# One mixer kernel, one change: half of the clamped differences through PSUM, one transpose bank instead of two, and another written order of the work

## The chip, the core and the metric

The kernel runs on one core of one Trainium2 chip. The metric is the device time of one execution in microseconds (us), lower is better. The engines of the core work side by side, each through its own list of instructions: PE (TensorE, matmuls; PEld is its weight load), DVE (VectorE), ACT (ScalarE), POOL (GpSimd) and SP (SyncE, which issues the DMAs). They meet only through semaphores.

## The reference

An input of 8 sequences of 256 tokens with 256 features is normalised to `xn`, and then `out = x + mamba_mixer(xn) + mlp(xn)`. The mixer, cut to what matters here (64 heads of 64 channels, state size 128):

```python
z, xbc, dt = split(xn @ W_in)              # 4096 + 4352 + 64 columns
xbc = silu(causal_conv1d(xbc, 4 taps))     # x: 4096 channels, B and C: 128 each
dt = softplus(dt + dt_bias); dA_cs = cumsum(dt * A)
L[i, j, h] = exp(dA_cs[i, h] - dA_cs[j, h])  for j <= i, else 0
Y[i, h] = sum_j (C_i . B_j) * L[i, j, h] * dt[j, h] * x[j, h]
y = (Y + D * x) * silu(z)
out_mixer = rmsnorm(y) * norm_w @ W_out
```

The MLP behind it is 6 blocks of two matmuls with a Gelu and a layernorm. It is the same before and after.

## The kernel before

Three stages follow each other. `prepare` (0 to about 72 us) normalises the input, computes B, C, the decay sums and `gmat`, the masked products C.B per sequence. `mix` (72 to 1040 us) is the stage that the change touches. `mlp` (from 1042 us) is the rest.

`mix` works through 32 channel tiles of 128 channels (2 heads each). A tile `c` has all 2048 tokens, in 4 blocks `b` of 512 tokens; a block is 2 sequences, and such a sequence is a *unit* `s` (0 or 1). For a tile the work is:

- PE `project_x`, `project_z` (8 products of 6 matmuls, L501) into the banks `pa0`, `pa1`.
- ACT `conv0` (L817) takes the x product out of PSUM, DVE `tap` (L517) adds three more taps per block from PSUM; then the bank is free and ACT `silu_x` (L826) finishes the block. ACT `silu_z` (L835) takes the z product out and frees its bank.
- PE `tokens` (L721) transposes a block of x into a bank `pt`, ACT `copy_tokens` (L862) copies it to `xtok`.
- DVE `exponents` (L943), per unit: 2 heads by 2 pieces of 256 and 128 columns, so 4 instructions, each `max(srow - stok, -CAP)`, SBUF to SBUF. ACT `decays` (L844) takes the exponential of the unit, POOL `times_g` (L657) multiplies it by `gmat`.
- PE `outputs` (L740), per unit: `xtok` times the unit's weights into `py`. DVE `add_dx` (L957) and `gate` (L971) finish the block; ACT `square` (L853) and POOL `add_square` (L666) gather the sum of squares.
- PE `output_rows` (L758), 4 calls per tile, multiplies the gated channels of a finished pair of tiles by `W_out` into `po`; DVE `add_rows` (L984) adds them to `acc`.

The order on each engine is written out by hand: a function `step(c)` per engine, called for c = -2 to 34. In a step an engine does parts of tile c, c-1 and c+1 in the order in which the calls stand; waits on semaphores inside the calls do the rest. An engine never passes an instruction that waits. Exp and Silu need different function tables on ACT; going from one to the other costs an ACT_TABLE_LOAD. `stok` (L923) is a small copy of the tile's columns of `tokpar`, made once per tile on DVE.

Two places of the code matter for the argument: `decays` and `silu_x`/`silu_z` in ACT's `step`, whose sequence sets how many table loads there are, and `outputs` in PE's `step`.

Of the kernel before, what the change touches and what calls it, by code (L numbers as in the profile page):

```python
# [28 lines left out]
P = 128  # L29
# [502 lines left out]
def mix(nc, w_xz, conv_par, d_par, w_out, w1, cs_dram, ident, xhi, xlo, acc, gmat, tokpar,  # L532
# [13 lines left out]
    with ExitStack() as ctx:  # L546
# [4 lines left out]
        stok = sb("stok", [P, 2, TILES, HPT])  # L551

        oraw = sb("oraw", [P, 2, DM + 1])
        osc = sb("osc", [P, 2, DM])
# [7 lines left out]
        pt = [ps(f"pt{i}") for i in range(2)]  # L562
        py = [ps(f"py{i}") for i in range(2)]
        po = [ps(f"po{i}") for i in range(2)]

# [67 lines left out]
        @block.gpsimd  # L633
        def _(pool):
            pool.memset(sqacc[:], 0.0).then_inc(pool_set, 1)
            pool.memset(onesq[:], 1.0).then_inc(pool_set, 1)
            pool.wait_ge(pool_set, 2)

            def w_lo(c):
                if not 2 <= c < NCT:  # L640
                    return
                t = tile_of(c)

# [24 lines left out]
            def step(c):  # L669
                add_square(c - 1, 1)  # L670
                times_g(c, 1, 0)
                times_g(c, 1, 1)
                times_g(c, 2, 0)
                add_square(c - 1, 2)
                times_g(c, 2, 1)
                add_square(c - 1, 3)
                times_g(c, 3, 0)
                w_lo(c + 2)
                times_g(c, 3, 1)
                times_g(c + 1, 0, 0)  # L680
                times_g(c + 1, 0, 1)
                add_square(c, 0)

            steps(step)

        @block.tensor
        def _(pe):
# [24 lines left out]
            def tokens(c, b):  # L712
# [47 lines left out]
                last.then_inc(o_done, 1)  # L760

            def step(c):
                project_x(c, 1)
                output_rows(c - 1, 0)
                outputs(c - 1, 0, 1)
                output_rows(c - 1, 1)
                project_x(c, 2)
                tokens(c - 1, 2)
                outputs(c - 1, 1, 0)
                outputs(c - 1, 1, 1)  # L770
                tokens(c - 1, 3)
                output_rows(c - 1, 2)
                project_x(c, 3)
                outputs(c - 1, 2, 0)
                output_rows(c - 1, 3)
                project_z(c, 0)
                outputs(c - 1, 2, 1)
                project_z(c, 1)
                project_z(c, 2)
                project_z(c, 3)  # L780
                outputs(c - 1, 3, 0)
                outputs(c - 1, 3, 1)
                tokens(c, 0)
                project_x(c + 1, 0)
                tokens(c, 1)
                outputs(c, 0, 0)

            steps(step)

            pe.wait_ge(sq_added, NB * NCT)  # L790
            for t in range(TILES):
                last = pe.matmul(pt[0][:, t:t + 1], sqacc[:, t * P:(t + 1) * P], onesq[:, 0:1],
                                 start=True, stop=True)
            last.then_inc(ms_done, 1)

# [1 line left out]
        def _(act):  # L797
# [57 lines left out]
            def copy_tokens(c, b):  # L855
                if not 0 <= c < NCT:
# [5 lines left out]
                act.copy(xtok[:, b % 2].rearrange("p t c -> p (t c)"), pt[b % 2][:]  # L862
                         ).then_inc(xtok_copied, 1)

            def scale_o(c):
# [7 lines left out]
                                   scale=oraw[:, e, DM:DM + 1]).then_inc(o_scaled, 1)  # L873

            def step(c):
                silu_z(c, 0)
                silu_x(c, 1)
                silu_x(c, 2)
                scale_o(c - 1)
                silu_z(c, 1)  # L880
                silu_z(c, 2)
                silu_x(c, 3)
                square(c - 1, 0)
                silu_z(c, 3)
                decays(c, 0, 0)
                decays(c, 0, 1)
                w_hi(c + 2)
                copy_tokens(c, 0)
                decays(c, 1, 0)
                decays(c, 1, 1)  # L890
                square(c - 1, 1)
                conv0(c + 1, 0)
                conv0(c + 1, 1)
                decays(c, 2, 0)
                copy_tokens(c, 1)
                conv0(c + 1, 2)
                copy_tokens(c, 2)
                decays(c, 2, 1)
                decays(c, 3, 0)
                square(c - 1, 2)  # L900
                copy_tokens(c, 3)
                square(c - 1, 3)
                conv0(c + 1, 3)
                decays(c, 3, 1)
                silu_x(c + 1, 0)

            steps(step)

# [1 line left out]
        def _(dve):  # L910
# [7 lines left out]
                conv_tap(dve, xt[:, t.par, cols(b)], pa[b % 2][:],  # L918
                         conv[:, t.par, TAPS - 1 - k:TAPS - k], k).then_inc(done, 1)

            def s_by_tokens(t):
                wait_past(dve, arg_done, SPB * NB * (t.c - 1))
                dve.tensor_copy(stok[:, t.par], tokpar[:, :, bass.ds(HPT * t.c, HPT)]  # L923
                                ).then_inc(stok_done, 1)

            def exponents(c, b, s):
                if not 0 <= c < NCT:
# [2 lines left out]

                m = SPB * (NB * t.c + b) + s
                half, i0 = b // 2, b % 2 * BLK + s * SEQ
                if b == 0 and s == 0:
                    s_by_tokens(t)
                    dve.wait_ge(stok_done, t.c + 1)
# [12 lines left out]
            def add_dx(c, b):  # L948
# [35 lines left out]
                dve.tensor_tensor(rows, po[i][:], rows, ALU.add).then_inc(o_added, 1)  # L984

            def step(c):
                add_rows(c - 1, 2)
                tap(c, 2, 2)
                tap(c, 3, 1)
                tap(c, 2, 3)  # L990
                tap(c, 3, 2)
                add_dx(c - 1, 1)
                tap(c, 3, 3)
                gate(c - 1, 1)
                add_rows(c - 1, 3)
                add_dx(c - 1, 2)
                gate(c - 1, 2)
# [5 lines left out]
                add_dx(c - 1, 3)  # L1003
                tap(c + 1, 0, 2)
                tap(c + 1, 1, 1)
                tap(c + 1, 1, 2)
                add_rows(c, 0)
                tap(c + 1, 0, 3)
                gate(c - 1, 3)
                exponents(c, 2, 0)  # L1010
                exponents(c, 2, 1)
                add_dx(c, 0)
                tap(c + 1, 1, 3)
                exponents(c, 3, 0)
                exponents(c, 3, 1)
                gate(c, 0)
                tap(c + 1, 2, 1)
                add_rows(c, 1)

            steps(step)  # L1020

            dve.wait_ge(ms_done, 1)
            dve.tensor_scalar(meansq[:], pt[0][:, 0:TILES], 1.0 / DI, EPS, ALU.mult,
                              ALU.add).then_inc(ms_copied, 1)

# [487 lines left out]
```

## Time and profile before

| | |
|---|---|
| median of 3 runs | 1621.53 us (1615.85 to 1621.72) |
| the profiled execution | 1617.42 us, its span 1615.4 us, mean granted TensorE clock 0.984 |
| busy share of the span | PE 93%, PEld 74%, DVE 74%, ACT 63%, POOL 58% |
| `mix` | about 72 to 1040 us, 32 tiles |
| one tile (step) in `mix` | 29.58 us, the mean of 31 |

In a timeline row "x8" means that eight neighbouring instructions of one kind are merged; the distance from its start to the start of the next row is the time which the engine gave to all eight.

### The profile page before, as it was taken

To read this page: it belongs to the slowest core of one execution; us is meant where nothing else is said; L and a number is where in the kernel's file an instruction comes from. 1 tells how busy PE (TensorE), PEld (TensorE's weight loads), DVE (VectorE), ACT (ScalarE), POOL (GpSimd) and SP (SyncE) were. 2 spreads that over 40 slices of the span, in tenths; PEclk is the share of its full clock that TensorE was granted. 3 is DMA by queue.
4 is the path that set the end of the run, shared out by engine and by line. 5 is a ranking of instruction groups with operands and counts; after the bars stand their busy time and mean duration, and the time that the engine had idled before them with its cause. 6 is when DMAs were issued, how large, how long until landed. Compare 5 with 4: busy or idle time off the path is not lost. (4 is left out here: it accounts for less than half of the span.)

```text
span 1615.4 us, 25959 instructions
## 1 busy us (share of the span) xinstructions
PE 1496.2 (93%) x8920; PEld 1200.1 (74%) x8920; DVE 1199.4 (74%) x2565; ACT 1019.4 (63%) x1620; POOL 938.8 (58%) x619
## 2 busy tenths in 40 slices
PE   6678999999999999999999998999999999999998
PEld 4556667666667666676666666789998998999988
DVE  7878788788788787887887887356676677677752
ACT  6557767767767677677676775366555555555542
POOL 4256677667766776776677667563535263343560
PEclk9889999999999999999999999899999999999999
DMA  4322223223232222222332311220100101020011
GB/s 134 105 85 99 66 86 99 66 85 99 70 103 76 92 86 72 92 86 73 97 93 70 108 65 53 71 74 1 63 1 27 36 0 62 0 75 0 0 53 40
DMA packets 50152, 107.52 MB, mean 67 GB/s; under 512 B 13249, under 2 KB 25793, under 8 KB 48449
## 3 DMA queue, kind: packets, MB, share of 16 engines
q1 hardware_dynamic: 50048, 106.21, 20.6%
q8 instruction: 57, 0.93, 0.2%
q14 instruction: 47, 0.38, 0.1%
HBM read 101.47 MB, written 4.72 MB: 66 GB/s over the span
## 5 line engine op out<-in xcount | busy, mean ns | idle before, releaser
L657 POOL TENSOR_TENSOR mix_dec<-mix_dec,gmat 128x768 f32<-128x768 f32 x256 | 466.6, 1836 | 222.4 <-ACT mix_dec L844 222.4
L517 DVE SCALAR_TENSOR_TENSOR xt<-mix_pa,conv,xt 128x510 f32<-128x510 f32 x372 | 263.9, 735 | 140.5 <-ACT xt L817 139.3
L1365 DVE TENSOR_TENSOR mlp_hlo<-mlp_h,mlp_hhi 128x512 fp32r<-128x512 f32 x192 | 208.2, 1086 | 184.8 <-ACT mlp_hhi L1297 184.6
L844 ACT ACTIVATE mix_dec<-mix_dec 128x768 f32<-128x768 f32 x256 | 209.6, 842 | 188.8 <-DVE mix_dec L943 188.3
L943 DVE TENSOR_SCALAR mix_dec<-srow,mix_stok 128x256 f32<-128x256 f32 (+1 forms) x1024 | 260.8, 327 | 27.0 <-PE mix_py L740 23.1
L740 PE MATMUL mix_py<-mix_dec,mix_xtok 128*64 128x256 f32 (+1 forms) x2048 | 213.3, 340 | 68.6 <-POOL mix_dec L657 36.9
L1292 ACT ACTIVATE mlp_h<-mlp_p,mlp_b1c 128x512 f32<-128x512 f32 x192 | 132.0, 687 | 203.7 <-PE mlp_p L501 197.8
L740 PEld LDWEIGHTS mix_py<-mix_dec,mix_xtok 128*64 128x64 f32 x2048 | 130.4, 138 | 166.8 <-ACT mix_xtok L862 81.9
L758 PE MATMUL mix_po<-mix_osc,mix_yg 128*128 128x256 f32 x1024 | 250.0, 389 | 0.0
L501 PE MATMUL mix_pa<-xhi,whi 128*128 128x512 f32 x496 | 220.7, 445 | 16.2 <-DVE xt L517 16.2
L1258 PE MATMUL mlp_p<-mlp_w2hi,mlp_hhi 128*128 128x256 f32 x768 | 218.7, 285 | 3.2 <-DVE acc L1424 3.2
L1260 PE MATMUL mlp_p<-mlp_w2hi,mlp_hlo 128*128 128x256 f32 x768 | 216.5, 282 | 0.0
L1259 PE MATMUL mlp_p<-mlp_w2lo,mlp_hhi 128*128 128x256 f32 x768 | 216.1, 281 | 0.0
L758 PEld LDWEIGHTS mix_po<-mix_osc,mix_yg 128*128 128x128 f32 x1024 | 188.9, 192 | 34.2 <-issue 10.3
L666 POOL TENSOR_TENSOR mix_sqacc<-mix_sqacc,mix_sq 128x512 f32<-128x512 f32 x128 | 163.1, 1286 | 72.2 <-ACT mix_sq L853 72.2
L501 PE MATMUL mix_pa<-xhi,wlo 128*128 128x512 f32 x496 | 197.8, 399 | 0.0
L501 PE MATMUL mix_pa<-xlo,whi 128*128 128x512 f32 x496 | 197.5, 398 | 0.0
L501 PE MATMUL mlp_p<-xhi,mlp_w1hi 128*128 128x512 f32 x384 | 153.5, 400 | 2.0 <-POOL mlp_w1lo L1153 2.0
L1258 PEld LDWEIGHTS mlp_p<-mlp_w2hi,mlp_hhi 128*128 128x128 f32 x768 | 144.6, 188 | 13.3 <-DVE mlp_hlo L1365 3.6
L501 PE MATMUL mlp_p<-xlo,mlp_w1hi 128*128 128x512 f32 x384 | 153.3, 399 | 0.0
L501 PE MATMUL mlp_p<-xhi,mlp_w1lo 128*128 128x512 f32 x384 | 153.1, 399 | 0.0
L1259 PEld LDWEIGHTS mlp_p<-mlp_w2lo,mlp_hhi 128*128 128x128 f32 x768 | 144.6, 188 | 6.1
(122 smaller groups left out, 2534.2 us busy)
## 6 DMA issues: line engine op xcount, KB each, us to landing
srow<-cs_rows SPq DMA_DIRECT2D x128, 512.0 KB, 4.6
wraw<-w_xz SPq DMA_DIRECT2D x32, 256.0 KB, 5.2
w1raw<-w SPq DMA_DIRECT2D x6, 1028.0 KB, 5.0
mlp_w2raw<-w SPq DMA_DIRECT2D x6, 1024.0 KB, 6.9
mix_oraw<-w_out SPq DMA_DIRECT2D x16, 257.0 KB, 2.7
prep_hid<-hidden SPq DMA_DIRECT2D x4, 512.0 KB, 5.6
xn_rows<-prep_hid SPq DMA_DIRECT2D x4, 512.0 KB, 2.9
mlp_res<-xn_rows SPq DMA_DIRECT2D x1, 2048.0 KB, 10.2
```

The lines of the kernel that those rows point to most:

```text
L501: last = pe.matmul(dst, w[:, k, :], x[:, k, cols], start=(i == 0), stop=(i == len(passes) - 1))
L517: return dve.scalar_tensor_tensor(d[:, :, k:SEQ], s[:, :, 0:SEQ - k], weight, d[:, :, k:SEQ], ALU.mult, ALU.add)
L657: pool.tensor_tensor(d, d, g, ALU.mult).then_inc(g_done, 1)
L666: pool.tensor_tensor(sqacc[:, cols(b)], sqacc[:, cols(b)], sq[:, b % 2, :], ALU.add).then_inc(sq_added, 1)
L740: last = pe.matmul(py[b % 2][hp, i], xtok[:, b % 2, 2 * s + j, hp], dec[:, b % 2, s, h, m], start=(j == 0), stop=(j == 1))
L758: last = pe.matmul(dst, yg[:, q % 2, e, r], osc[:, e, :], start=(e == 0), stop=(e == 1))
L844: act.activation(d, d, ACT.Exp, scale=-1.0).then_inc(dec_done, 1)
L943: last = dve.tensor_scalar(dec[:, b % 2, s, h, k], srow[:, half, h, i], stok[:, t.par, tile, h:h + 1], -CAP, ALU.subtract, ALU.max)
L1258: pe.matmul(dst, hhi[:, j, k], w2hi[:, j, :], start=(j == 0), stop=False)
L1259: pe.matmul(dst, hhi[:, j, k], w2lo[:, j, :], start=False, stop=False)
L1260: last = pe.matmul(dst, hlo[:, j, k], w2hi[:, j, :], start=False, stop=(j == KH - 1))
L1365: dve.tensor_tensor(hlo[:, j, :], h[:, j % 4, :], hhi[:, j, :].bitcast(F32), ALU.subtract).then_inc(hlo_done, 1)
```

## The change

- The buffer `stok` and its copy are gone; `exponents` reads the scalar from `tokpar` directly.
- Unit 0 of each block keeps the `tensor_scalar` (subtract, then max with the constant). Unit 1 uses a `scalar_tensor_tensor` whose third operand is a column of a PSUM bank `floor`, filled once with -CAP and broadcast along the row.
- `pt` is one bank instead of two (the freed bank is `floor`), so `tokens` of a block waits for `copy_tokens` of the block just before it, not of the one before that.
- The calls in `step` stand in another order on PE, ACT, DVE and POOL.

```diff
-                wait_past(pe, xtok_copied, n - 1)
+                wait_past(pe, xtok_copied, n)
...
-                    last = pe.transpose(pt[b % 2][:, k % TPB * P:(k % TPB + 1) * P],
+                    last = pe.transpose(pt[:, k % TPB * P:(k % TPB + 1) * P],
...
-            def s_by_tokens(t):
-                wait_past(dve, arg_done, SPB * NB * (t.c - 1))
-                dve.tensor_copy(stok[:, t.par], tokpar[:, :, bass.ds(HPT * t.c, HPT)]
-                                ).then_inc(stok_done, 1)
+            dve.memset(floor[:], -CAP).then_inc(floor_set, 1)
+            dve.wait_ge(floor_set, 1)
...
-                        last = dve.tensor_scalar(dec[:, b % 2, s, h, k], srow[:, half, h, i],
-                                                 stok[:, t.par, tile, h:h + 1], -CAP,
-                                                 ALU.subtract, ALU.max)
+                        if s == 0:
+                            last = dve.tensor_scalar(dec[:, b % 2, s, h, k], srow[:, half, h, i],
+                                                     tokpar[:, tile, HPT * c + h:HPT * c + h + 1], -CAP,
+                                                     ALU.subtract, ALU.max)
+                        else:
+                            last = dve.scalar_tensor_tensor(
+                                dec[:, b % 2, s, h, k], srow[:, half, h, i],
+                                tokpar[:, tile, HPT * c + h:HPT * c + h + 1],
+                                floor[:, 0:1].broadcast_to([P, k.stop - k.start]), ALU.subtract, ALU.max)
...
             def step(c):
-                silu_z(c, 0)
-                silu_x(c, 1)
+                decays(c - 1, 2, 1)
+                decays(c - 1, 3, 0)
...
```

**The order on PE**, before, from the transposes of block 2 to the next x product (`pt` transposes, `py` outputs of a unit in four rows, `po` output rows):

```order
L721 MATMUL mix_pt0<-ident,xt 128x128 x4
L740 MATMUL mix_py1<-mix_dec,mix_xtok 64x256 x2
L740 MATMUL mix_py1<-mix_dec,mix_xtok 64x128 x2
L740 MATMUL mix_py1<-mix_dec,mix_xtok 64x256 x2
L740 MATMUL mix_py1<-mix_dec,mix_xtok 64x128 x2
L721 MATMUL mix_pt1<-ident,xt 128x128 x4
L758 MATMUL mix_po0<-mix_osc,mix_yg 128x256 x4
```

The same place after:

```order
L741 MATMUL mix_py1<-mix_dec,mix_xtok 64x256 x2
L741 MATMUL mix_py1<-mix_dec,mix_xtok 64x128 x2
L722 MATMUL mix_pt<-ident,xt 128x128 x4
L741 MATMUL mix_py1<-mix_dec,mix_xtok 64x256 x2
L741 MATMUL mix_py1<-mix_dec,mix_xtok 64x128 x2
```

A row pair 64x256, 64x128 is one unit. Before, the units of blocks 1 and 3 stand next to each other in pairs; after, every unit stands alone, with transposes or a product between the two of a block.

**The order on ACT**, before, from the first exponential of a tile back through the Silu group:

```order
L844 ACTIVATE mix_dec<-mix_dec 128x768
L826 ACT_TABLE_LOAD
L826 ACTIVATE xt<-xt 128x512
L835 ACTIVATE zt<-mix_pa0 128x512
L826 ACTIVATE xt<-xt 128x512 x2
```

After, at the same place of a step, where Exp (`mix_dec`) and Silu (`xt`) alternate:

```order
L845 ACTIVATE mix_dec<-mix_dec 128x768 x2
L818 ACTIVATE xt<-mix_pa1,conv 128x512
L827 ACT_TABLE_LOAD
L827 ACTIVATE xt<-xt 128x512
L845 ACT_TABLE_LOAD
L845 ACTIVATE mix_dec<-mix_dec 128x768
L827 ACT_TABLE_LOAD
L827 ACTIVATE xt<-xt 128x512
```

There are 4 table loads in a step after, and 2 before. And behind the last `silu_z` of a tile, before:

```order
L844 ACT_TABLE_LOAD
L844 ACTIVATE mix_dec<-mix_dec 128x768 x2
L804 CAST whi<-wraw 128x512
L862 COPY mix_xtok<-mix_pt0 128x512
L844 ACTIVATE mix_dec<-mix_dec 128x768 x2
L853 ACTIVATE mix_sq<-mix_yg 128x512
L817 ACTIVATE xt<-mix_pa0,conv 128x512
```

and after:

```order
L845 ACT_TABLE_LOAD
L845 ACTIVATE mix_dec<-mix_dec 128x768
L854 ACTIVATE mix_sq<-mix_yg 128x512
L818 ACTIVATE xt<-mix_pa0,conv 128x512
L845 ACTIVATE mix_dec<-mix_dec 128x768
```

`conv0` of the next tile's first block (the row with `conv`) stands behind four exponentials before, and behind one after.

On DVE the first `tap` of the next tile follows behind the exponents of the blocks 0 and 1, before and after. The exponents of block 3 of a tile, which stood ahead of the next tile's first tap of block 2, stand at the start of the next step now, behind `gate` of block 0.

## Rows read from the trace of the kernel before

**Rows 1.** Windows: stretch, us, busy us by engine (PE, PEld, DVE, ACT, POOL), PE clock, DMA.

```profile
400.00:600.00 200.00, 185.22 (x1084) 137.46 (x1083) 162.57 (x389) 141.35 (x217) 137.59 (x88) 1.00 0.26 81
1100.00:1600.00 500.00, 496.82 (x3204) 448.51 (x3203) 336.26 (x580) 272.76 (x473) 218.21 (x149) 1.00 0.08 27
```

**Rows 2.** DVE timeline, `gate` of block 0 of the tiles 0 and 31.

```profile
95.35 0.68 DVE L971 TENSOR_TENSOR mix_yg<-mix_py,zt 128x512 f32<-128x512 f32 x1
...
1012.38 0.68 DVE L971 TENSOR_TENSOR mix_yg<-mix_py,zt 128x512 f32<-128x512 f32 x1
```

**Rows 3.** Waits of PE, 400 to 900 us: us in total, times, longest.

```profile
PE mix_py L740 <- POOL mix_dec L657: 18.6, 17, 1.1
PE mix_py L740 <- ACT mix_xtok L862: 13.0, 17, 0.8
PE mix_pa L501 <- DVE xt L517: 4.4, 17, 0.3
```

**Rows 4.** Waits of DVE, same stretch.

```profile
DVE xt L517 <- ACT xt L817: 77.5, 17, 4.6
```

**Rows 5.** ACT timeline behind the last `silu_z` of a tile.

```profile
522.65 1.28 ACT L844 ACT_TABLE_LOAD   x1
...
528.41 0.76 ACT L817 ACTIVATE xt<-mix_pa,conv 128x512 f32<-128x512 f32 x1
```

**Rows 6.** PE timeline of one step.

```profile
530.96 0.87 PE L740 MATMUL mix_py<-mix_dec,mix_xtok 128*64 128x256 f32 x8
531.76 1.99 PE L758 MATMUL mix_po<-mix_osc,mix_yg 128*128 128x256 f32 x8
534.01 0.50 PE L501 MATMUL mix_pa<-xhi,whi 128*128 128x512 f32 x1 [0.26 <-DVE xt L517]
...
534.80 0.39 PE L501 MATMUL mix_pa<-xhi,whi 128*128 128x512 f32 x1
...
536.88 1.52 PE L740 MATMUL mix_py<-mix_dec,mix_xtok 128*64 128x256 f32 x16 [0.77 <-ACT mix_xtok L862]
538.33 0.66 PE L721 MATMUL mix_pt<-ident,xt 128*128 128x128 f32 x4
```

**Rows 7.** DVE timeline: taps, then exponents of two units.

```profile
512.78 2.69 DVE L517 SCALAR_TENSOR_TENSOR xt<-mix_pa,conv,xt 128x508 f32<-128x508 f32 x4
515.40 0.74 DVE L957 SCALAR_TENSOR_TENSOR mix_py<-xt,mix_dcol,mix_py 128x512 f32<-128x512 f32 x1
...
534.47 1.91 DVE L943 TENSOR_SCALAR mix_dec<-srow,mix_stok 128x256 f32<-128x256 f32 x8
536.31 0.75 DVE L957 SCALAR_TENSOR_TENSOR mix_py<-xt,mix_dcol,mix_py 128x512 f32<-128x512 f32 x1
```

**Rows 8.** Groups by shape: count, busy us, mean ns, idle before.

```profile
L844 ACT ACT_TABLE_LOAD x32 | 41.1, 1283 | 0.8 <-PEq L114 0.3
L1377 DVE TENSOR_TENSOR mlp_u<-mlp_p,mlp_res 128x256 f32<-128x256 f32 x80 | 28.2, 414 | 0.3
L971 DVE TENSOR_TENSOR mix_yg<-mix_py,zt 128x512 f32<-128x512 f32 x128 | 87.0, 680 | 1.1
L923 DVE COPY mix_stok<-tokpar 128x32 f32<-128x32 f32 x32 | 28.2, 880 | 3.1 <-PEq L114 3.1
```

**Rows 9.** Timelines: L943 at the start of `mix`; POOL; L943 beside POOL.

```profile
74.08 7.00 DVE L943 TENSOR_SCALAR mix_dec<-srow,mix_stok 128x256 f32<-128x256 f32 x16
...
512.22 1.82 POOL L657 TENSOR_TENSOR mix_dec<-mix_dec,gmat 128x768 f32<-128x768 f32 x1
514.00 1.27 POOL L666 TENSOR_TENSOR mix_sqacc<-mix_sqacc,mix_sq 128x512 f32<-128x512 f32 x1
...
536.43 1.82 POOL L657 TENSOR_TENSOR mix_dec<-mix_dec,gmat 128x768 f32<-128x768 f32 x1 [1.92 <-ACT mix_dec L844]
...
537.79 0.61 DVE L943 TENSOR_SCALAR mix_dec<-srow,mix_stok 128x256 f32<-128x256 f32 x1
```

**Rows 10.** All instructions of L943: duration ns min/median/max, first and last start us.

```profile
L943 DVE TENSOR_SCALAR mix_dec<-srow,mix_stok x1024: 269/338/1967, 74.1 to 1012.2; 128x256 f32<-128x256 f32 x171
```

More of the change, by code:

```diff
@@ L550, in mix @@
         dcol = sb("dcol", [P, 2, 1])
-        stok = sb("stok", [P, 2, TILES, HPT])
         oraw = sb("oraw", [P, 2, DM + 1])
@@ L561, in mix @@
         pa = [ps(f"pa{i}") for i in range(2)]
-        pt = [ps(f"pt{i}") for i in range(2)]
+        pt = ps("pt")
+        floor = ps("floor")
         py = [ps(f"py{i}") for i in range(2)]
@@ L574, in mix @@
         xtok_copied = sem("xtok_copied")
+        floor_set = sem("floor_set")
         arg_done = sem("arg_done")
@@ L669, in step @@
             def step(c):
-                add_square(c - 1, 1)
+                times_g(c, 0, 1)
                 times_g(c, 1, 0)
@@ L673, in step @@
                 times_g(c, 2, 0)
+                times_g(c, 2, 1)
                 add_square(c - 1, 2)
-                times_g(c, 2, 1)
                 add_square(c - 1, 3)
@@ L679, in step @@
                 times_g(c, 3, 1)
+                add_square(c, 0)
                 times_g(c + 1, 0, 0)
-                times_g(c + 1, 0, 1)
-                add_square(c, 0)
+                add_square(c, 1)
             steps(step)
@@ L762, in step @@
             def step(c):
-                project_x(c, 1)
+                tokens(c - 1, 0)
                 output_rows(c - 1, 0)
+                outputs(c - 1, 0, 0)
+                tokens(c - 1, 1)
                 outputs(c - 1, 0, 1)
+                project_x(c, 2)
                 output_rows(c - 1, 1)
-                project_x(c, 2)
+                outputs(c - 1, 1, 0)
                 tokens(c - 1, 2)
-                outputs(c - 1, 1, 0)
                 outputs(c - 1, 1, 1)
+                project_x(c, 3)
                 tokens(c - 1, 3)
                 output_rows(c - 1, 2)
-                project_x(c, 3)
                 outputs(c - 1, 2, 0)
                 output_rows(c - 1, 3)
+                outputs(c - 1, 2, 1)
                 project_z(c, 0)
-                outputs(c - 1, 2, 1)
                 project_z(c, 1)
@@ L781, in step @@
                 outputs(c - 1, 3, 0)
+                project_x(c + 1, 0)
                 outputs(c - 1, 3, 1)
[L783 to L786, printed above, removed]
+                project_x(c + 1, 1)
             steps(step)
@@ L791, in _ @@
             for t in range(TILES):
-                last = pe.matmul(pt[0][:, t:t + 1], sqacc[:, t * P:(t + 1) * P], onesq[:, 0:1],
+                last = pe.matmul(pt[:, t:t + 1], sqacc[:, t * P:(t + 1) * P], onesq[:, 0:1],
                                  start=True, stop=True)
@@ L861, in copy_tokens @@
                 wait_past(act, y_done, SPB * (n - 1))
-                act.copy(xtok[:, b % 2].rearrange("p t c -> p (t c)"), pt[b % 2][:]
+                act.copy(xtok[:, b % 2].rearrange("p t c -> p (t c)"), pt[:]
                          ).then_inc(xtok_copied, 1)
@@ L875, in step @@
             def step(c):
+                decays(c - 1, 2, 1)
+                decays(c - 1, 3, 0)
+                conv0(c, 3)
+                silu_x(c, 0)
+                decays(c - 1, 3, 1)
+                silu_x(c, 1)
                 silu_z(c, 0)
-                silu_x(c, 1)
+                copy_tokens(c - 1, 3)
+                silu_z(c, 1)
                 silu_x(c, 2)
-                scale_o(c - 1)
-                silu_z(c, 1)
-                silu_z(c, 2)
                 silu_x(c, 3)
                 square(c - 1, 0)
+                silu_z(c, 2)
                 silu_z(c, 3)
                 decays(c, 0, 0)
+                scale_o(c - 1)
+                square(c - 1, 1)
+                conv0(c + 1, 0)
                 decays(c, 0, 1)
-                w_hi(c + 2)
+                conv0(c + 1, 1)
                 copy_tokens(c, 0)
                 decays(c, 1, 0)
+                w_hi(c + 2)
+                copy_tokens(c, 1)
                 decays(c, 1, 1)
-                square(c - 1, 1)
-                conv0(c + 1, 0)
-                conv0(c + 1, 1)
                 decays(c, 2, 0)
-                copy_tokens(c, 1)
+                square(c - 1, 2)
+                square(c - 1, 3)
+                copy_tokens(c, 2)
                 conv0(c + 1, 2)
[L897 to L905, printed above, removed]
             steps(step)
@@ L932, in exponents @@
                 half, i0 = b // 2, b % 2 * BLK + s * SEQ
-                if b == 0 and s == 0:
-                    s_by_tokens(t)
-                    dve.wait_ge(stok_done, t.c + 1)
                 if b % 2 == 0 and s == 0:
@@ L986, in step @@
             def step(c):
+                gate(c - 1, 0)
+                exponents(c - 1, 3, 0)
+                exponents(c - 1, 3, 1)
+                tap(c, 2, 1)
+                tap(c, 3, 1)
+                tap(c, 2, 2)
                 add_rows(c - 1, 2)
-                tap(c, 2, 2)
-                tap(c, 3, 1)
                 tap(c, 2, 3)
                 tap(c, 3, 2)
+                tap(c, 3, 3)
                 add_dx(c - 1, 1)
-                tap(c, 3, 3)
-                gate(c - 1, 1)
                 add_rows(c - 1, 3)
                 add_dx(c - 1, 2)
+                gate(c - 1, 1)
                 gate(c - 1, 2)
@@ L1002, in step @@
                 tap(c + 1, 0, 1)
-                add_dx(c - 1, 3)
                 tap(c + 1, 0, 2)
                 tap(c + 1, 1, 1)
-                tap(c + 1, 1, 2)
                 add_rows(c, 0)
                 tap(c + 1, 0, 3)
+                add_dx(c - 1, 3)
+                tap(c + 1, 1, 2)
+                add_dx(c, 0)
+                tap(c + 1, 1, 3)
                 gate(c - 1, 3)
@@ L1011, in step @@
                 exponents(c, 2, 1)
[L1012 to L1017, printed above, removed]
                 add_rows(c, 1)
@@ L1022, in _ @@
             dve.wait_ge(ms_done, 1)
-            dve.tensor_scalar(meansq[:], pt[0][:, 0:TILES], 1.0 / DI, EPS, ALU.mult,
+            dve.tensor_scalar(meansq[:], pt[:, 0:TILES], 1.0 / DI, EPS, ALU.mult,
                               ALU.add).then_inc(ms_copied, 1)
```

1 line of the change is left out of this document (removed).

## The prediction

> **What bounds the kernel now.** I read the windows first. In the steady middle of `mix` PE is busy for 185.22 of 200 us, DVE 162.57, ACT 141.35, POOL 137.59, all at the granted clock of 1.00; in `mlp` PE is busy for 496.82 of 500 us [rows 1]. So `mlp` has nothing to give and is not touched; what a reordering can win lies in `mix`, and on PE it is the part in which PE is idle.
>
> Then the timeline of DVE: `gate` of block 0 comes at 95.35 us for tile 0 and at 1012.38 for tile 31 [rows 2]: 917.03/31 = 29.58 us a step. The pattern repeats, so one step stands for all.
>
> Then the waits. In 17 steps PE waits for POOL's weights 18.6 us, for the ACT copy of the transposed tokens 13.0 us, for DVE's taps 4.4 us [rows 3]: 1.09 + 0.76 + 0.26 = 2.12 us a step, and PE works for 29.58 - 2.12 = 27.46 us. DVE waits 77.5/17 = 4.56 us a step in one place, for `conv0` [rows 4]. Neither is full: the step is a loop through several engines. It goes through ACT: behind the last `silu_z` the table load starts at 522.65, and `conv0` of the next tile, which releases DVE's taps and through them PE's third x product, starts only at 528.41, 5.76 us later [rows 5], behind four exponentials, a weight copy, a token copy and a square.
>
> **The change part by part.**
>
> *PE.* The same instructions. An outputs unit alone takes 531.76 - 530.96 = 0.80 us until the next kind starts; two side by side take 538.33 - 536.88 = 1.45 us [rows 6]. The new order splits two such pairs in a step. Each split costs 2 x 0.80 - 1.45 = 0.15 us at least; a unit entered behind another kind starts up to as late as the first matmul behind a wait is long, 0.50 against 0.39 us [rows 6], and a unit's change on both sides makes it 0.29 at most. So 0.30 to 0.58 us more. Against that, the restarts behind the three waits (0.11 us each by the same rows, 0.3 in all) go if the waits go. PE's own work is then 27.46 + 0.30 - 0.30 = 27.46 us at the least and 27.46 + 0.58 = 28.04 us at the most. I take 27.9, near the upper end, as some tenths of waiting will remain.
>
> *DVE, unit 1 through PSUM.* No row shows this operation. The tap, also a `scalar_tensor_tensor` with one PSUM operand, gives 515.40 - 512.78 = 2.62 us for four, 0.655 each at 510 columns [rows 7]. How the time falls with width comes from two DVE operations of one kind: 680 ns at 512 columns, 414 at 256 [rows 8], so 0.266 us for 256 columns. That makes 0.655 - 0.266 = 0.389 us for 256 and 0.256 for 128 columns, and 2 x (0.389 + 0.256) = 1.29 us for the unit. A unit of today takes (536.31 - 534.47)/2 = 0.92 us [rows 7]. Bounds: not below 0.92, as nothing in the form makes it faster than today's two-at-once rate; not above 4 x 0.655 = 2.62, as if the width saved nothing. I take 1.29, as it rests on the row of the same operation. 4 units: +1.48 us a step. The `stok` copy goes: 0.88 to 0.93 us with its hand-over [rows 8]. DVE is busy 162.57/200 x 29.58 = 24.0 us a step now [rows 1], and 24.0 + 1.48 - 0.93 = 24.6 us then. 27.9 leaves it 3.3 us free, so the dearer form is covered; at the upper bound, 2.62, DVE would need 24.6 + 5.3 = 29.9 us and the cover is gone. Reading the scalar from `tokpar` instead of `stok` changes a single column's address: 0, bounded by 0.05 us on the 32 small instructions of a step, which the same free time covers.
>
> *ACT.* Four table loads a step in place of two, 1.283 us each [rows 8]: 2.57 us. ACT is busy 141.35/200 x 29.58 = 20.9 us [rows 1], so 23.5 us of 27.9. The loads stand ahead of the wait of their ACTIVATE, so they are run while ACT would wait for DVE anyway, if that operand is late. What pays for them: behind `silu_z` only a load (1.28), one exponential (0.84), every second step `osc` (about 0.8) and a square (0.5) stand ahead of `conv0`: 2.6 to 3.5 us in place of 5.76. So the taps come 2.3 to 3.1 us sooner, which is more than PE's 2.12 us of waiting. That is why I think the loop opens.
>
> *One transpose bank.* `tokens` of a block now waits for the copy of the block before. The calls are spread out: between the transposes of blocks 0 and 1 stand output rows (2.2 us, 531.76 to about 534.0 with a unit's restart) and a unit (0.8) [rows 6], together 3.0 us, while the copy needs 0.57 us plus what is queued ahead of it on ACT. The tightest place that I find is this copy of block 0: laid end to end, `silu_z` 0.6, load 1.28, exponential 0.75, `osc` 0.8, square 0.5, `conv0` 0.68, exponential 0.75, `conv0` 0.68, copy 0.57 is 6.6 us behind the last z product, and PE asks for it behind a unit, a product, a unit, a product, the transposes and the output rows, 0.9 + 1.5 + 0.9 + 1.4 + 0.5 + 1.8 = 7.0 us. With some 0.05 us at each hand-over about 0.2 us are left. In every second step there is no `osc`, and 1.0 us is left. If it comes late, PE loses just that.
>
> *POOL* keeps its work, 137.59/200 x 29.58 = 20.3 us a step [rows 1]. SP keeps its order; the loads of `srow` for a tile are issued when its predecessor's exponents are done, and those of block 3, which come later now, are still most of a step ahead of their reader.
>
> *The edges of `mix`.* At the start the 16 exponents took 7.00 us [rows 9] where four units make 4 x 0.92 = 3.7; the rest, 3.3 us, went beside POOL. Half of them cannot be held up in that way now but are dearer by 0.37 a unit; between 0 and 3.3 I take 2 us saved.
>
> **Sum.** 31 steps x (29.58 - 27.9) = 52.1 us, and the start 2. Together 54 us. From the profiled execution, 1617.42 (span 1615.4 and 2.0 around it), that gives 1563 us. The median of the runs shown is 4 us above it, so by the median it is 1567. I say 1565, between the two, 3.5% faster.
>
> **The port.** In the step the first exponent of a unit started at 537.79 and took 0.61 us in place of 0.34; POOL's product ran from 536.43 to 538.25 [rows 9]. Over the stage the same instruction takes 338 ns in the median and up to 1967 [rows 10], a whole product of POOL. The four taps at 512.78, with one operand in PSUM, took their 0.655 us each while POOL worked at a product from 512.22 and a sum from 514.00 to 515.27 [rows 7, 9]. So unit 1 in the new form escapes POOL, and unit 0 does not. The Trainium skill (SBUF — State Buffer, Who interferes with whom) states it as a lock: a two-port DVE operation and a GpSimd one exclude each other for the whole instruction, and the second one blocks fully. The trace agrees, with 0.61 us and with 1967 ns. By that rule the new order would be slower if each unit 0 met the start of a POOL product; that case is the third below.
>
> **The rivals.**
>
> 1. *PE full, 27.5 to 28.1 us a step* (chance 0.75): 1565 us, own range 1552 to 1574.
>
> 2. *The table loads reach PE* (0.10). For it: they nearly double, and two stand between an exponential and a Silu on which products wait. Against it: 4.4 us of slack on ACT. If one load of the four comes through, the step is 27.9 + 1.28 = 29.2 us, and 31 x 0.38 + 2 = 14 us are saved: 1604 us.
>
> 3. *DVE waits for POOL* (0.08), the case on the slow side. Every unit 0, on DVE, starts when a product of POOL has just begun and is held for its 1.83 us: 24.6 + 4 x 1.83 = 31.9 us a step, +2.3 us for 31 steps, 1690 us. It decides from (29.58 - 24.6)/4 = 1.25 us a unit. For it: the longest rows of L943. Against it: in the steady step before one of eight units meets POOL, and loses 0.27 us; and in the new order the exponents of a block precede POOL's work on it.
>
> 4. *The PSUM form is dear* (0.07): at the upper bound DVE needs 29.9 us, 31 x 0.32 = 10 us more than today, less the 2 at the start: 1625 us, no change.
>
> **How the numbers follow.** No change that a measurement of this kernel can tell is within 0.5%, 8 us. Cases 1 and 2 are faster: 0.75 + 0.10 = 0.85. Case 4 is the same: 0.07. Slower: 0.08. The range should leave out 2 in 10: 1550 to 1595 takes all of case 1 and steps up to 28.9 us, short of case 2.
>
> **What would show it.** In the profile after: the distance between the gates of neighbouring tiles 27.9 us; PE's waits on POOL and on the token copy below 0.5 us a step; DVE's 4.56 us wait on `conv0` nearly gone, and other waits of 3 us in all on PE's outputs in its place; the new exponents at about 0.48 and 0.35 us each (0.39 and 0.26 from start to start); 4 table loads a step; unit 0 held by POOL for 1 us a step or less. I am wrong if PE still waits 1 us or more in a step, and the engine that it waits for tells which rival it is.

## The result and the profile after

The changed kernel takes 1553.22 us (median of 4 runs, 1552.79 to 1558.28) against 1620.45 us for the kernel before: a ratio of 0.960, 95% interval 0.957 to 0.963. The profiled execution has a span of 1551.4 us, 64 us less than before, at a mean granted clock of 0.988.

Where the 64 us went, by `gate` of block 0 of the tiles 0 and 31 on DVE:

```profile
88.87 0.68 DVE L973 TENSOR_TENSOR mix_yg<-mix_py,zt 128x512 f32<-128x512 f32 x1
...
949.35 0.68 DVE L973 TENSOR_TENSOR mix_yg<-mix_py,zt 128x512 f32<-128x512 f32 x1
```

The 31 steps between them take 860.48 us, 27.76 each, against 917.03 and 29.58 in [rows 2]: 56.5 us. The first gate comes 6.5 us sooner (88.87 against 95.35), and what follows the last one is 1.0 us shorter (602.1 against 603.0).

The windows of the steady stretch of `mix` and of `mlp`, the columns as in [rows 1]:

```profile
400.00:600.00 200.00, 200.00 (x1150) 145.29 (x1149) 181.26 (x402) 170.55 (x246) 150.91 (x95) 1.00 0.29 93
...
1036.00:1536.00 500.00, 497.42 (x3207) 448.93 (x3206) 339.05 (x581) 272.83 (x473) 218.24 (x149) 1.00 0.08 27
```

PE has no idle time left in `mix` (200.00 of 200, before 185.22). `mlp` is as it was. A list of PE's matmul waits from 350 to 850 us is empty, where [rows 3] had three entries; what waits instead is DVE and ACT:

```profile
ACT mix_dec L845 <- DVE mix_dec L940: 50.3, 18, 2.8
...
DVE mix_dec L944 <- PE mix_py L741: 25.1, 18, 1.4
DVE mix_dec L940 <- PE mix_py L741: 18.0, 18, 1.0
...
DVE xt L517 <- ACT xt L818: 1.5, 9, 0.2
```

DVE waited 4.56 us a step for `conv0` before [rows 4] and 1.5/18 = 0.08 us now; it waits for PE instead, 43.1/18 = 2.4 us a step. A wait on the engine that sets the pace is where spare time should lie.

ACT behind the last `silu_z`, the counterpart of [rows 5]:

```profile
547.42 1.28 ACT L845 ACT_TABLE_LOAD   x1
548.72 0.84 ACT L845 ACTIVATE mix_dec<-mix_dec 128x768 f32<-128x768 f32 x1
549.47 0.61 ACT L854 ACTIVATE mix_sq<-mix_yg 128x512 f32<-128x512 f32 x1
549.99 0.76 ACT L818 ACTIVATE xt<-mix_pa,conv 128x512 f32<-128x512 f32 x1
```

From the load to `conv0` it is 2.57 us, where it was 5.76; in every second step `osc` stands between as well, and it is 3.37 us (from 575.19).

The exponents on DVE (timeline: unit 0 plain, then unit 1 through PSUM), and POOL in the same microseconds:

```profile
547.62 1.01 DVE L940 TENSOR_SCALAR mix_dec<-srow,tokpar 128x256 f32<-128x256 f32 x4 [0.98 <-PE mix_py L741]
550.02 1.39 DVE L944 SCALAR_TENSOR_TENSOR mix_dec<-srow,tokpar,mix_floor 128x256 f32<-128x256 f32 x4 [1.39 <-PE mix_py L741]
551.33 2.18 DVE L517 SCALAR_TENSOR_TENSOR xt<-mix_pa,conv,xt 128x510 f32<-128x510 f32 x3
```

```profile
549.64 1.85 POOL L658 TENSOR_TENSOR mix_dec<-mix_dec,gmat 128x768 f32<-128x768 f32 x1 [2.13 <-ACT mix_dec L845]
551.45 1.28 POOL L667 TENSOR_TENSOR mix_sqacc<-mix_sqacc,mix_sq 128x512 f32<-128x512 f32 x1
552.68 3.62 POOL L658 TENSOR_TENSOR mix_dec<-mix_dec,gmat 128x768 f32<-128x768 f32 x2
```

The four PSUM instructions take 551.33 - 550.02 = 1.31 us although POOL is at work from 549.64 on. Keep this place in mind: unit 1 of block 1, written (1,1) below, at the head of a *train* of POOL instructions, four that follow each other without a pause (a product, a sum, two products). All instructions of the new form, and the table loads, as groups with mean ns:

```profile
L944 DVE SCALAR_TENSOR_TENSOR mix_dec<-srow,tokpar,mix_floor 128x256 f32<-128x256 f32 x256 | 121.2, 473 | 41.8 <-PE mix_py L741 41.8
...
L944 DVE SCALAR_TENSOR_TENSOR mix_dec<-srow,tokpar,mix_floor 128x128 f32<-128x128 f32 x256 | 86.9, 339 | 0.0
...
L845 ACT ACT_TABLE_LOAD x63 | 80.8, 1283 | 1.4 <-PEq L114 0.3
L827 ACT ACT_TABLE_LOAD x62 | 79.5, 1283 | 1.1
```

### The profile page after: what moved, and what is told of

Read it like the earlier page. It is cut to its first block and busy times, and to the rows that moved or that the text cites. A ratio compares the mean times of both kernels' runs of the same rounds, so it can differ in the third digit from the quotient of the medians.

```text
span 1551.4 us, 25991 instructions
## 1 busy us (share of the span) xinstructions
PE 1500.6 (97%) x8920; PEld 1189.6 (77%) x8920; DVE 1230.6 (79%) x2534; ACT 1097.4 (71%) x1682; POOL 941.6 (61%) x619
## 5 line engine op out<-in xcount | busy, mean ns | idle before, releaser
L1367 DVE TENSOR_TENSOR mlp_hlo<-mlp_h,mlp_hhi 128x512 fp32r<-128x512 f32 x192 | 215.5, 1125 | 181.5 <-ACT mlp_hhi L1299 181.2
L759 PE MATMUL mix_po<-mix_osc,mix_yg 128*128 128x256 f32 x1024 | 245.2, 383 | 0.0
L741 PE MATMUL mix_py<-mix_dec,mix_xtok 128*64 128x256 f32 (+1 forms) x2048 | 224.7, 341 | 10.8 <-POOL mix_dec L658 5.2
L741 PEld LDWEIGHTS mix_py<-mix_dec,mix_xtok 128*64 128x64 f32 x2048 | 125.3, 137 | 124.3 <-issue 72.2
L501 PE MATMUL mix_pa<-xhi,whi 128*128 128x512 f32 x496 | 212.7, 429 | 7.5 <-DVE xt L517 4.4
L944 DVE SCALAR_TENSOR_TENSOR mix_dec<-srow,tokpar,mix_floor 128x256 f32<-128x256 f32 (+1 forms) x512 | 177.0, 406 | 41.8 <-PE mix_py L741 41.8
L667 POOL TENSOR_TENSOR mix_sqacc<-mix_sqacc,mix_sq 128x512 f32<-128x512 f32 x128 | 162.0, 1277 | 57.5 <-ACT mix_sq L854 57.5
L940 DVE TENSOR_SCALAR mix_dec<-srow,tokpar 128x256 f32<-128x256 f32 (+1 forms) x512 | 150.1, 355 | 32.0 <-PE mix_py L741 31.9
```

The costliest lines, as they stand in the source:

```text
L501: last = pe.matmul(dst, w[:, k, :], x[:, k, cols], start=(i == 0), stop=(i == len(passes) - 1))
L741: last = pe.matmul(py[b % 2][hp, i], xtok[:, b % 2, 2 * s + j, hp], dec[:, b % 2, s, h, m], start=(j == 0), stop=(j == 1))
L759: last = pe.matmul(dst, yg[:, q % 2, e, r], osc[:, e, :], start=(e == 0), stop=(e == 1))
L944: last = dve.scalar_tensor_tensor(dec[:, b % 2, s, h, k], srow[:, half, h, i], tokpar[:, tile, HPT * c + h:HPT * c + h + 1], floor[:, 0:1] ...
L1367: dve.tensor_tensor(hlo[:, j, :], h[:, j % 4, :], hhi[:, j, :].bitcast(F32), ALU.subtract).then_inc(hlo_done, 1)
```

## The experiments

Eleven kernels. The table has the ratio to the kernel before with its 95% interval, and the step, the mean distance of the gates of block 0 from tile 4 to tile 26.

| | median us | ratio | step us |
|---|---|---|---|
| before | 1617 to 1620 | 1 | 29.57 |
| after | 1553.22 | 0.960 (0.957 to 0.963) | 27.77 |
| e1 new order, all plain | 1744.35 | 1.080 (1.078 to 1.082) | 34.13 |
| e2 the same, two banks | 1748.25 | 1.081 (1.079 to 1.082) | 34.13 |
| e3 old order, new form and bank | 1639.9 | 1.014 (1.013 to 1.016) | 30.22 |
| e4 two table loads | 1553.72 | 0.961 (0.959 to 0.963) | 27.77 |
| e5 PSUM form in both units | 1552.6 | 0.959 (0.956 to 0.961) | 27.86 |
| e6 `conv0` late | 1616.13 | 0.999 (0.997 to 1.000) | 29.80 |
| e7 two pairs of units together | 1543.61 | 0.954 (0.951 to 0.956) | 27.39 |
| e8 four pairs together | 1539.48 | 0.950 (0.948 to 0.953) | 27.18 |
| e9 unit (1,1) plain | 1743.05 | 1.076 (1.073 to 1.080) | 34.13 |
| e10 only unit (1,1) through PSUM | 1592.61 | 0.983 (0.980 to 0.987) | 28.78 |
| e11 before, `conv0` early | 1654.79 | 1.021 (1.017 to 1.025) | 30.73 |

### Order and form apart: e1, e2, e3

e1 undoes the form and keeps the order and the one bank:

```diff
-                        if s == 0:
+                        if s >= 0:
                             last = dve.tensor_scalar(...
```

> The changed kernel, but unit 1 keeps the plain tensor_scalar too; order and single transpose bank as changed. Theory A (the form matters because it lets the exponents run beside POOL): with the new order the unit 1 exponents meet POOL products, the step rises from 27.77 to between 28.6 and 29.6 us, the time to 1580 to 1610 us, and L943's kind shows durations of up to 1.9 us in unit 1. Rival B (the order alone carries the gain, the form is incidental and only costs DVE 1.48 us a step): the step stays 27.8 us and the time 1553 us within 4 us.

Measured: 1744 us, slower than before by 8%. Theory A has the direction; its price was far too low. The step is 34.13 us. DVE, POOL and PE of e1, in one step, each from a timeline:

```profile
514.51 6.42 DVE L940 TENSOR_SCALAR mix_dec<-srow,tokpar 128x256 f32<-128x256 f32 x4 [1.39 <-PE mix_py L741]
520.85 2.17 DVE L517 SCALAR_TENSOR_TENSOR xt<-mix_pa,conv,xt 128x510 f32<-128x510 f32 x3
...
517.25 1.92 DVE L940 TENSOR_SCALAR mix_dec<-srow,tokpar 128x256 f32<-128x256 f32 x1
...
519.10 1.83 DVE L940 TENSOR_SCALAR mix_dec<-srow,tokpar 128x128 f32<-128x128 f32 x1
```

```profile
514.12 1.85 POOL L658 TENSOR_TENSOR mix_dec<-mix_dec,gmat 128x768 f32<-128x768 f32 x1 [2.12 <-ACT mix_dec L845]
515.93 1.32 POOL L667 TENSOR_TENSOR mix_sqacc<-mix_sqacc,mix_sq 128x512 f32<-128x512 f32 x1
517.21 3.64 POOL L658 TENSOR_TENSOR mix_dec<-mix_dec,gmat 128x768 f32<-128x768 f32 x2
```

```profile
519.54 0.87 PE L741 MATMUL mix_py<-mix_dec,mix_xtok 128*64 128x256 f32 x8
524.33 0.80 PE L501 MATMUL mix_pa<-xhi,whi 128*128 128x512 f32 x1 [3.91 <-DVE xt L517]
524.92 0.63 PE L501 MATMUL mix_pa<-xlo,whi 128*128 128x512 f32 x1
525.35 0.63 PE L501 MATMUL mix_pa<-xhi,wlo 128*128 128x512 f32 x1
```

The four exponents of unit (1,1), 0.92 us of work, take 6.34 us (514.51 to 520.85). There are four POOL instructions in the time, and each exponent ends just behind the end of one of POOL's: the third starts at 517.25 behind the POOL start of 517.21 and lasts its 1.9 us, the fourth starts at 519.10 and does so again. The train of POOL lets in one plain exponent between two of its instructions. The taps stand behind them, PE behind the taps, for 3.91 us. The second loss is in the clock, in the windows of e1:

```profile
500.00:520.00 20.00, 20.00 (x114) 14.45 (x114) 15.97 (x27) 17.97 (x26) 15.77 (x11) 1.00 0.20 66
520.00:524.00 4.00, 0.41 (x6) 0.14 (x2) 3.96 (x6) 1.08 (x2) 2.66 (x2) 0.82 0.00 0
524.00:530.00 6.00, 5.67 (x14) 4.32 (x14) 5.33 (x14) 1.55 (x3) 0.64 (x1) 0.55 0.59 165
...
524.40:529.30 4.90, 4.90 (x12) 3.88 (x13) 4.90 (x13) 0.85 (x2) 0.00 (x0) 0.50 0.59 161
```

PE is busy for 0.41 us of the 4 from 520 to 524, and in the 6 us behind it the granted clock is 0.55, almost all at 1.2 GHz: a matmul there takes 0.63 us where it takes 0.40 at 2.4 GHz, and what counts, the distance from one start to the next, is 0.43 us (524.92 to 525.35) where it is 0.23 at 2.4 GHz (514.73 to 514.96). A mean of 0.55 over 6 us is 5.4 us at 0.50, so the slow stretch ends at 529.4. PE works in it from 524.33 on, 5.1 us, and does what takes 5.1 x 0.23/0.43 = 2.7 us at 2.4 GHz. So the 6.36 us of a step (34.13 - 27.77) are 3.9 us of waiting and, by this estimate, 2.4 us of slow clock behind it. No run parts the two. In the changed kernel PE never idles so long, and the clock in the middle of `mix` is 1.00.

e2 takes the order alone, with two banks:

```diff
-                wait_past(pe, xtok_copied, n)
+                wait_past(pe, xtok_copied, n - 1)
```

> The new order alone: plain tensor_scalar in both units and two transpose banks. Theory: the bank is worth nothing, so this is the same as the run with one bank and all plain within 3 us. Rival: the single bank costs PE up to 0.3 us a step, then this one is up to 9 us faster than that run.

The step is 34.13 us, e1's to the hundredth, and the times are 4 us apart, just over the 3 us that I had allowed, with the two-bank kernel the slower one. So the second bank is worth nothing in this order with all units plain. In that loop PE waits 3.9 us a step for something else; for the changed kernel itself it is the empty list of PE's waits above that shows that the single bank costs nothing.

e2 and e3 have one part of the change more: the `stok` copy, 0.9 us of DVE a step, is gone in both.

e3 puts the four `step` functions of before back, with the new form and one bank:

> The new form of unit 1, no copy of the scalars and one transpose bank, but the order of before on all engines. Theory: the old loop is set through ACT and DVE, DVE gets 0.55 us longer a step and a unit's exponents 0.37 us later, so the step is 29.6 to 30.1 us and the time 1618 to 1635 us. Rival: half of the gain comes from the form, escape from POOL at 0.27 us a step included; then it is 1585 to 1600 us.

Measured 1640 us, 1.4% slower than before and 5 us beyond my range; the step is 0.65 us longer. The waits of e3, 400 to 900 us:

```profile
PE mix_pt L722 <- ACT mix_xtok L863: 42.2, 32, 1.4
```

Twice in a step PE's transposes wait for the token copy, 1.3 us each, 2.6 us in all, a wait that the kernel before did not have. It is the only wait of PE in this run and takes the place of the 2.12 us of [rows 3], so it is longer by 0.5 of the 0.65 us. The single bank is thus a rival to the form as the cause of this loss, and I did not run the form without the bank: what the form alone does in the old order is open. Order and form are no sum all the same: the form with the single bank is +23 us, the order +131 us, and all of it together about -65 us.

### Which unit: e9, e10

Their edits are `if s == 0 or b == 1:` and `if s == 0 or b != 1:` in place of `if s == 0:`.

> The changed kernel with one of its four PSUM units plain again, unit 1 of block 1, the one whose four exponents took 6.42 us in the run with all plain, because four instructions of POOL follow each other there. Theory (each plain instruction is let in between two of POOL's and so waits for one of them): this unit alone brings nearly the whole loss: PE waits for the taps about 3.9 us a step, and the step is 33 to 34.2 us, 1715 to 1750 us. Rival (all units lose a little): below 29.5 us a step, under 1607 us.

> The counterpart: the PSUM form in unit 1 of block 1 alone, plain in the other seven units. Theory: no train of POOL instructions stands beside the others, they lose at most 0.5 us each, which DVE's free time covers: a step of 27.8 to 28.3 us, 1553 to 1570 us. Rival (the loss is spread over the units): 30 us or more, above 1620 us.

e9 is e1 again, 1743 us and 34.13 us: one unit of eight, made plain, brings the whole loss of 190 us. e10 protects only that one and is 27 us faster than before. But it misses its range, 1592.6 against at most 1570, so the other units are not free either. Its timelines show where:

```profile
523.46 5.07 DVE L940 TENSOR_SCALAR mix_dec<-srow,tokpar 128x256 f32<-128x256 f32 x8
528.46 2.04 DVE L517 SCALAR_TENSOR_TENSOR xt<-mix_pa,conv,xt 128x510 f32<-128x510 f32 x3
```

```profile
522.39 1.83 POOL L658 TENSOR_TENSOR mix_dec<-mix_dec,gmat 128x768 f32<-128x768 f32 x1 [1.81 <-ACT mix_dec L845]
525.31 1.86 POOL L658 TENSOR_TENSOR mix_dec<-mix_dec,gmat 128x768 f32<-128x768 f32 x1 [1.09 <-ACT mix_dec L845]
527.13 2.56 POOL L667 TENSOR_TENSOR mix_sqacc<-mix_sqacc,mix_sq 128x512 f32<-128x512 f32 x2
```

The eight exponents of block 3 need 5.00 us in place of 1.84, held three times until an instruction of POOL has ended; in POOL's pause, from 524.22 to 525.31, they run freely. No train of four is needed for a loss. PE's wait for the taps is 16.5 us in 18 steps, 0.9 a step, the 1.0 us by which the step is longer.

### The dear form everywhere: e5

`if s < 0:`, so that all units go through PSUM.

> The changed kernel with the PSUM form in both units of a block. Theory (what costs is the port, not the PSUM form, and PE sets the step): DVE gets 1.48 us more a step and is never held by POOL; 25.2 us + 1.5 - 0.5 us of holding = 26.2 of 27.77 us, so the step stays 27.77 us and the time 1553 us within 5 us. Rival (the plain form in unit 0 is needed, since the dear form makes DVE the bound): a step of 28.2 us or more, 1566 us or more.

1552.6 us and 27.86 us: as the theory says. DVE is busy for 188.14 of 200 us and still is not the bound. Keeping unit 0 plain is neither needed nor harmful here.

### The table loads: e4

```diff
-                silu_x(c, 0)
                 decays(c - 1, 3, 1)
+                silu_x(c, 0)
```

> The changed kernel with decays(c-1,3,1) ahead of silu_x(c,0), so 2 table loads in a step in place of 4: ACT gets 2.57 us less work a step. Theory: PE sets the step and the loads are hidden, so the step stays 27.77 us and the time 1553 us within 4 us. Rival: the loads hold the chain, then the time falls by up to 31 x 0.5 = 15 us.

1553.7 us and 27.77 us: 62 loads fewer, 82 us less work on ACT (busy 1015.1 in place of 1097.4 us), and no change in the time. What ACT saves goes into its wait for PE's z products, 57.5 us in 18 steps (350 to 850 us) where the changed kernel has 8.6: 2.7 us a step more, for 2.57 us of loads.

### What opened the loop: e6, e11

e6 takes the changed kernel and puts `conv0` of blocks 0 and 1 back behind two more exponentials:

```diff
-                conv0(c + 1, 0)
                 decays(c, 0, 1)
-                conv0(c + 1, 1)
                 copy_tokens(c, 0)
                 decays(c, 1, 0)
+                conv0(c + 1, 0)
+                conv0(c + 1, 1)
```

> The changed kernel with conv0 of the next tile's blocks 0 and 1 put behind decays(c,1,0) again, about 2.5 us later. Theory (the loop was opened by conv0 and the taps coming earlier): PE waits for the taps, the step rises to 29 to 30 us and the time to 1590 to 1620 us. Rival (there is slack, another of the moves opened the loop): below 28.2 us a step, under 1566 us.

1616 us and 29.80 us: all of the gain is gone by this one edit. PE waits for the taps in it, 27.9 us in 17 steps:

```profile
DVE xt L517 <- ACT xt L818: 45.4, 17, 2.7
...
PE mix_pa L501 <- DVE xt L517: 27.9, 17, 1.6
```

e11 makes the same kind of move in the kernel before:

```diff
                 decays(c, 0, 0)
+                conv0(c + 1, 0)
                 decays(c, 0, 1)
...
                 square(c - 1, 1)
-                conv0(c + 1, 0)
                 conv0(c + 1, 1)
```

> The kernel before with one edit: conv0(c+1,0) moved from behind decays(c,1,1) and square to behind decays(c,0,0), 4.1 us earlier on ACT. Theory (the loop of before has several arms, and the place of conv0 opens only one): DVE's wait for conv0 shrinks by up to 4 us, but each exponential behind it comes 0.68 us later and PE then waits for POOL and the copy instead: 29.0 to 30.1 us a step, 1600 to 1635 us. Rival (this move is the change): 28.2 us or less, under 1575 us.

It is 2.1% slower than before, and 20 us beyond my range. Its waits, 350 to 850 us; then the gates of block 0 of three tiles in a row; then PE and the clock in the step from 500.43:

```profile
DVE xt L517 <- ACT xt L817: 88.3, 32, 4.6
...
PE mix_py L740 <- ACT mix_xtok L862: 40.0, 32, 2.2
```

```profile
500.43 0.68 DVE L971 TENSOR_TENSOR mix_yg<-mix_py,zt 128x512 f32<-128x512 f32 x1
...
531.63 0.68 DVE L971 TENSOR_TENSOR mix_yg<-mix_py,zt 128x512 f32<-128x512 f32 x1
...
561.39 0.68 DVE L971 TENSOR_TENSOR mix_yg<-mix_py,zt 128x512 f32<-128x512 f32 x1
```

```profile
518.06 1.55 PE L740 MATMUL mix_py<-mix_dec,mix_xtok 128*64 128x256 f32 x8 [2.21 <-ACT mix_xtok L862]
...
518.10:521.40 3.30, 3.30 (x12) 2.24 (x13) 0.28 (x1) 1.91 (x3) 3.30 (x4) 0.50 0.66 210
```

PE waits for the token copy 40.0/16 = 2.5 us a step, where it was 0.76 [rows 3], since the copy stands behind the `conv0` that was moved. The x product of block 1 stands behind that wait, so its `conv0` is late, and DVE waits for it up to 4.6 us. The theory holds in kind: `conv0` early is needed (e6) but does not do it alone (e11). Which of the other moves (the copy, the exponentials, PE's products) it needs beside it, no run parts.

The rows show why the time rose by 35 us and not by up to 15. Steps of two lengths alternate, two of 31.2 us (531.63 - 500.43) and one of 29.76 (561.39 - 531.63). The short ones are 0.2 us longer than the 29.57 of before and lie in the range that I expected. Every step has a wait of PE of 2.21 us for the token copy; in the long ones the granted clock is 0.50 for 3.4 us from about the end of that wait on, and in the short ones it stays at 1.00. So the slow clock costs 1.44 us in a long step, 2 x 1.44/3 = 0.96 us a step in the mean, 31 x 0.96 = 30 us. It makes up most of the rise, and the waits as such little of it.

### A better version: e7, e8

In e7 the transposes that stand between two outputs units move ahead of both, for the blocks 0 and 1; e8 does it for all four blocks (there with `output_rows` and `project_x` in the place of the transposes).

```diff
-                outputs(c - 1, 0, 0)
                 tokens(c - 1, 1)
+                outputs(c - 1, 0, 0)
                 outputs(c - 1, 0, 1)
```

> The changed kernel with the transposes between the two outputs units of blocks 0 and 1 moved ahead of them, so that both pairs of units stand together. Theory (PE sets the step, and each split of a pair costs 0.15 to 0.29 us): the step falls by 0.3 to 0.58 us to 27.2 to 27.5 us, the time to 1535 to 1544 us. Rival (the single transpose bank needs the spacing, the transposes wait for the copy): PE waits again for the copy and the step stays at 27.8 us or rises, 1553 us or more.

> As the run before, and the pairs of blocks 2 and 3 put together too: four pairs in a step. Theory: four times 0.15 to 0.29 us, so a step of 26.6 to 27.2 us and 1517 to 1535 us. Rival: DVE, at 25.2 us of work a step and with waits of its own, or POOL's products become late; then PE waits over 0.3 us a step and the time is not below that of the run with two pairs.

e7 takes 1543.6 us: in its steady steps PE is busy for 200.00 of 200 us, and the step is 27.34 to 27.36 us for most tiles. That is 0.42 us less than 27.77 for two splits, 0.21 us each. Two units together in e7, and apart with the transposes between them in the changed kernel (PE timelines, from the output rows to the next product):

```profile
546.77 1.89 PE L759 MATMUL mix_po<-mix_osc,mix_yg 128*128 128x256 f32 x8
...
549.03 1.52 PE L741 MATMUL mix_py<-mix_dec,mix_xtok 128*64 128x256 f32 x16
550.48 0.50 PE L501 MATMUL mix_pa<-xhi,whi 128*128 128x512 f32 x1
```

```profile
551.85 1.89 PE L759 MATMUL mix_po<-mix_osc,mix_yg 128*128 128x256 f32 x8
553.67 0.87 PE L741 MATMUL mix_py<-mix_dec,mix_xtok 128*64 128x256 f32 x8
...
555.06 0.87 PE L741 MATMUL mix_py<-mix_dec,mix_xtok 128*64 128x256 f32 x8
555.86 0.50 PE L501 MATMUL mix_pa<-xhi,whi 128*128 128x512 f32 x1
```

From start to the next start, the two units take 1.45 us together and 2 x 0.80 = 1.60 apart. The whole piece, with the same rows and transposes in it, takes 3.71 us in e7 and 4.01 in the changed kernel: 0.30 us for a split, twice what the units alone show. Of these 0.60 us a step only 0.42 reach the step; the 24 products in a row take 0.2 us longer in e7 (541.62 - 535.63 = 5.99 against 546.70 - 540.89 = 5.81), and PE's weight load waits there for `silu_z` to free the bank, 6.3 us in 18 steps.

e8 has 1539.5 us, 0.950 of before and the fastest of all. Its runs (1537.1 to 1540.5) lie all below those of e7 (1543.3 to 1546.5), though the intervals of the two ratios touch. It misses its range of 1517 to 1535 us, and the rival is right in part: PE is busy for 197.98 of 200 us, and DVE waits for `conv0` again, 24.3/19 = 1.3 us a step. I take it that the next gain would have to come from ACT's order; no run tries it.

## Why the prediction was right

It forecast 1565 us with 1550 to 1595; measured were 1553, 3 us inside the lower end. By its own steps:

- *PE is what the step can fall to, and its waits are what can be won.* Right. The step is PE's own work now, 27.77 us; predicted were 27.46 to 28.04, and I took 27.9 for "some tenths of waiting". No waiting was left, so 31 x 0.13 = 4 us more were won. The split of a pair, 0.15 to 0.29, is 0.30 us by e7's rows, the upper end, of which 0.21 reach the step.
- *The loop is opened by `conv0`.* Right as far as it was said: 2.57 and 3.37 us behind the load (2.6 to 3.5 predicted, 5.76 before), and e6 shows that the gain hangs on it. It is not the only arm, as e11 shows.
- *The new form costs 1.29 us a unit.* 1.31 us. DVE is busy 181.26/200 x 27.77 = 25.2 us a step (24.6 predicted). POOL holds unit 0 for 0.5 us of it (544.06 to 545.27 and 533.90 to 535.01, 0.3 and 0.2 us more than 0.92), but 0.27 of that was in the 24.0 of before, so this is 0.2 of the 0.6 us; the rest I have not traced. Its cover was as wide as said; e5 doubles the cost and the time stays.
- *The table loads are hidden.* Right (e4), though not as said. In the steady steps no load falls into a wait for DVE: the ACTIVATE behind each starts 0.02 us after it ends (547.42 + 1.28, then 548.72). What hides the loads is that ACT has time left before the z products come, as e4 shows.
- *The single bank costs nothing.* Right in this order: PE has no wait in the changed kernel. In the old order a wait on it appears (e3).
- *The start of `mix` saves 2 us.* It saved 6.5, and the end 1.0. This is the largest mis-sized term, and its reason was wrong: the first 16 exponents take 8.35 us now (73.59 to 81.94) where they took 7.00, as unit 0 of block 1 is still held (76.74 to 80.64 us for four exponents) and the new form is dearer. What the start saves is the order: the gate of block 0 no longer stands behind the exponents of block 3 (91.89 to 95.35 before), and DVE's waits of 1.58 and 1.28 us for `conv0` and of 1.09 us for PE before that gate are gone.
- *Rival 3, the port.* The mechanism was right, its price and its point wrong, and this would have misled whoever chose the form by it. I priced a held unit at one POOL product, 1.83 us, and the whole case at 31.9 us a step. A unit beside a train of POOL instructions is held once for each of its four exponents, 5.4 us (6.34 - 0.92), and one such unit is enough for 34.13 us a step. The start of the stage in the kernel before hinted at it (16 exponents in 7.00 us, [rows 9]); I used that row only for the edge. I had treated the escape from POOL as worth about 0.27 us a step; in the new order it is worth 6.36. That no plain unit stands at the train was not worked out, and in this the forecast had luck: the reason given, that a block's exponents precede POOL's work on it, is no cover, as the products of the train are POOL's work on the units before. And that the engines meet only through semaphores, as I wrote at the start, is too narrow: the plain exponents stand still for POOL's instructions with no semaphore between them.

The rule of the Trainium skill (SBUF — State Buffer, Who interferes with whom), that the second of the two blocks for the whole instruction of the first, is what e1 shows, instruction by instruction. That every small DVE instruction in a row pays anew beside a train is from e1's timeline. The same section of the Trainium skill says that a DVE instruction with at most one SBUF input, outside the two-port modes, does not contend with GpSimd; the trace agrees, with 1.31 us for the unit beside POOL at 550.02. No run gives the new form its third operand from SBUF, so that it is the PSUM operand and not the kind of instruction that helps is not shown here.

## What to carry to other kernels

Judge a reordering and a change of an instruction's form together: here the order without the form was slower by 131 us, the form (with the single bank) in the old order by 23, and together they won 65. Before making two engines overlap more, look for small SBUF-to-SBUF DVE instructions that will then run beside long GpSimd ones; a form that is slower by itself but is not held by GpSimd (here one with an operand in PSUM) can be the cheaper one. Look at the granted clock of each step before you explain a longer one by its waits: in e11 the clock behind a wait of 2.2 us cost most of the time lost. And when PE has no idle time left, count its changes from one kind of matmul to another: putting like units side by side gave a further 10 to 14 us.

## What the runs showed of the hardware

- A train of POOL instructions lets one plain (SBUF to SBUF `tensor_scalar`) DVE instruction in between each two of its own: 4 instructions of 0.92 us together took 6.34 us beside four of POOL's (e1). The PSUM form at the same place took 1.31 us, wholly beside the train's first product.
- PE busy for 0.41 of 4 us was followed by 6 us at a mean granted clock of 0.55, with matmuls of 0.63 in place of 0.40 us and starts 0.43 in place of 0.23 us apart (e1); in e11 a wait of PE of 2.21 us was followed by 3.4 us at 0.50 in two steps of three, which made these steps 1.44 us longer. I had not expected that a DVE and POOL conflict would be paid a second time on PE.
- Splitting a pair of outputs units by another kind of matmul costs PE 0.30 us (4.01 against 3.71 us for the same work), of which the two units themselves show 0.15 (e7).
